# Experts' first layer: one 256-column operand for the high weights, halves added on VectorE, four PSUM banks in a ring

## The chip, the cores and the metric

One core of a Trainium2 chip runs the whole program. The metric is device time in microseconds; the program is launched once and its time is that of the core.

## The reference

Four transformer-like layers work on 2 sequences, 16 batches of 113 tokens with 256 features in all (1808 tokens). Only two of its parts are touched, the two mixtures of experts:

```python
# L0_ffn: 15 experts, 3 picks for each token, F = 256
logits = xt @ gate_w.T; scores = softmax(logits); topk_w, topk_idx = top_k(scores, 3)
h = einsum('td,efd->etf', xt, fc1_w) + fc1_b      # 512 outputs per expert
xh, g = h[..., :F], h[..., F:]
a = gelu(g, approximate=False) * xh * geglu_mult
yexp = einsum('etf,edf->etd', a, fc2_w) + fc2_b   # then weighted and summed over the picks
# L3_ffn: 8 experts, 1 pick, F = 1024
h = relu(xt @ w1[e] + b1[e]); y = h @ w2[e] + b2[e]
```

The kernel computes in pairs of fp16 numbers (a high part and the rest), three products for each product of the reference: high by high, high by low, low by high.

## The kernel before

`program` runs stage after stage; each is a block in which five engines run side by side, tied by semaphores, and a barrier stands between stages. A router stage sorts the tokens by expert into blocks of 128 rows, each of one expert. `stage_experts` then runs over the blocks. It is used twice: as m0x for L0 (57 blocks, NF = 4 chunks of 128 hidden units in the first layer, FH = 2 in the second, gelu, with the preparation of later weights, `PrepareShared`, laid beside it) and as m3x for L3 (23 blocks, NF = FH = 8, relu, no preparation).

For one block n:

- GpSimd (POOL) copies the block's row numbers (`idx`), gathers its 128 rows with an indirect DMA (`xg`, four buffers), and copies the expert's bias (`b1`, two buffers). It does so in a hardware loop, with registers in its waits.
- TensorE (PE) turns the gathered rows in four transposes into `pt` (`turn`), multiplies the first layer (`first`) into `ph` and the second (`second`) into `py`.
- ScalarE (ACT) copies `pt` to `xb` (`take_tokens`), makes `gate` from the upper half of `ph` with gelu (`take_gate`, m0x alone) and rounds the activation to fp16 (`high`; in m3x it reads `ph` with relu and bias).
- VectorE (DVE) makes the activation `a` from `ph` (`product`), the fp16 rest of it (`low`), and the output with its bias (`output`).
- SyncE (SP) fetches the output bias and stores the block's output to `m_out`.

The order on each engine is written out by hand. PE's in turn n is: turn(n+3), first(n+2), second(n). ACT's is, in m0x: high(n+1), take_tokens(n+3), take_gate(n+2), then a piece of the preparation; in m3x take_tokens(n+3), high(n+2). DVE's is: low(n+1), product(n+2), output(n), preparation (in m3x product(n+2), low(n+2), output(n)). So in m0x high(n+2) is the next thing that ACT does after take_gate(n+2), and `product(n+2)` on DVE stands between the two.

`ph` has two buffers of [128, NF, 128] floats. `first` waits for the xb of its block and for `taken` (a_ready or lo_ready) of the block two before. Its weights' place depends on the expert number, a value in a register, so each weight operand has an address that is worked out by the engine while it runs:

```python
def first(self, e, k, f):
    at, n = 2 * (k * self.NF + f) * 128, KC * self.NF * 256
    return [w[:].rearrange("p e k n -> p (e k n)").bitcast(mybir.dt.uint8)[:, bass.ds(e * n + at, 256)].bitcast(F16)
            for w in (self.w1_hi, self.w1_lo)]
```

Each f has two k steps (KC = 2), and `mm3` (lines 458 to 460) makes three matmuls of 128 columns for each: high weights by high tokens, high weights by low tokens, low weights by high tokens. Each matmul has a weight load of its own.

Of the kernel before, what the change touches and what calls it, by code (L numbers as in the profile page):

```python
# [6 lines left out]
F16 = mybir.dt.float16  # L7
I32 = mybir.dt.int32
U32 = mybir.dt.uint32
ALU = mybir.AluOpType  # L10
# [6 lines left out]
D = 256  # L17
# [139 lines left out]
class Ternary:  # L157
# [5 lines left out]
    def __init__(self, st, tag, mats, floor, depth):  # L163
# [5 lines left out]
        self.tot = st.ps(f"{tag}_tot", [128, M])  # L169
# [18 lines left out]
    def total(self, pe, i):  # L188
        pe.wait_ge(self.ones_set, 1)
        pe.wait_ge(self.summed, i + 1)  # L190
        pe.matmul(self.tot[:, i:i + 1], self.ones[:], self.asum[:, i:i + 1], start=True, stop=True).then_inc(self.totals, 1)

    def thresholds(self, dve, i):
        dram, out, scale = self.mats[i]
        dve.wait_ge(self.totals, i + 1)
        self.floor(dve, scale, self.tot[:, i:i + 1], 1.0 / (128 * dram.shape[1])).then_inc(self.scaled, 1)
# [92 lines left out]
class PrepareShared:  # L289
# [4 lines left out]
    def __init__(self, st, d, w, g):  # L294
# [6 lines left out]
                          lambda dve, out, tot, inv: dve.tensor_scalar(out, tot, inv, 1e-6, ALU.mult, ALU.add), 1)  # L301
# [19 lines left out]
    def on_tensor(self, pe, n):  # L321
        if n in (23, 40):
            self.bg.total(pe, (n - 23) // 17)
# [14 lines left out]
    def on_vector(self, dve, n):  # L338
# [16 lines left out]
        for i in range(2):  # L355
# [3 lines left out]
            if b == 5:  # L359
                self.bg.thresholds(dve, i)  # L360
# [1190 lines left out]
def stage_experts(nc, core, m, d, prepare=None):  # L1551
# [4 lines left out]

    N, NF, FH = m.blocks, m.NF, m.FH
    with Stage(nc, m.name + "x") as st:
# [3 lines left out]
        xb = [st.sb(f"xb{p}", [128, 2 * KC, 128], F16) for p in two]  # L1562
# [6 lines left out]
        ph = [st.ps(f"ph{p}", [128, NF, 128]) for p in two]  # L1569
        py = [st.ps(f"py{p}", [128, 512]) for p in two]  # L1570
        idx_ready, gathered, turned = ([st.sem(f"{n}{p}") for p in four] for n in ("idx_ready", "gathered", "turned"))
        xb_ready, h_ready, b1_ready, gate_ready, a_ready, hi_ready, lo_ready, y_ready, b2_landed, y_out, stored = (
            [st.sem(f"{n}{p}") for p in two] for n in (
                "xb_ready", "h_ready", "b1_ready", "gate_ready", "a_ready", "hi_ready", "lo_ready", "y_ready",
                "b2_landed", "y_out", "stored"))

        taken = a_ready if m.gelu else lo_ready
        if prepare is not None:
            prepare = prepare(st)
        with nc.Block() as block:  # L1580
            @block.gpsimd
            def _(pool):
# [3 lines left out]
                def gather(at):  # L1586
                    p, before = at.of(4)

                    wait_alone(pool, core, turned[p], before)
                    pool.tensor_copy(idx[p][:], m.ids[:, bass.ds(at.j, 1)]).then_inc(idx_ready[p], 1)  # L1590
                    wait_alone(pool, core, idx_ready[p], before + 1)
# [4 lines left out]
                def bias(at):  # L1596
                    p, before = at.of(2)
                    e = pool.value_load(m.expert[0:1, bass.ds(at.j, 1)], min_val=0, max_val=m.E - 1)

                    wait_alone(pool, core, taken[p], before)  # L1600
                    pool.tensor_copy(b1[p][:], m.b1[:, bass.ds(e, 1), :]).then_inc(b1_ready[p], 1)

                def step(at):
                    gather(at + 3)
                    bias(at)

                for n in range(3):
                    gather(At(0, n))
                steps(pool, N - 3, step)
                for n in range(N - 3, N):  # L1610
                    bias(At(0, n))

            @block.tensor
            def _(pe):
# [19 lines left out]
                def first(n, e):  # L1634
                    p = n % 2
                    pe.wait_ge(xb_ready[p], n // 2 + 1)

                    need(pe, taken[p], n // 2)
                    for f in range(NF):
                        for k in range(KC):  # L1640
                            last = mm3(pe, ph[p][:, f, :], *m.first(e, k, f), xb[p][:, k, :], xb[p][:, KC + k, :],
                                       k == 0, k == KC - 1)
                    last.then_inc(h_ready[p], 1)

                def second(n, e):
                    p, r = n % 2, n % 3

                    need(pe, y_out[p], n // 2)
                    pe.wait_ge(hi_ready[p], n // 2 + 1)
# [14 lines left out]
                for n in range(N):  # L1664
# [6 lines left out]
                    if prepare is not None:  # L1671
                        prepare.on_tensor(pe, n)

            @block.scalar
            def _(act):
                def take_tokens(n):
# [3 lines left out]
                    need(act, h_ready[p], n // 2)  # L1680
                    act.activation(xb[p][:].rearrange("p c n -> p (c n)"), pt[p][:, 0:2 * KC * 128],  # L1681
                                   ACT.Copy).then_inc(xb_ready[p], 1)

                def take_gate(n):
# [10 lines left out]
                def high(n):  # L1695
# [4 lines left out]
                    if m.gelu:  # L1700
                        act.wait_ge(a_ready[p], n // 2 + 1)
                        act.activation(a_hi[r][:], act32[p][:], ACT.Copy).then_inc(hi_ready[p], 1)
                        return
                    act.wait_ge(h_ready[p], n // 2 + 1)
                    act.wait_ge(b1_ready[p], n // 2 + 1)
                    for f in range(FH):
                        ins = act.activation(a_hi[r][:, f, :], ph[p][:, f, :], ACT.Relu, bias=b1[p][:, 0, f:f + 1])  # L1707
                    ins.then_inc(hi_ready[p], 1)

                take_tokens(0)  # L1710
                take_tokens(1)
                if m.gelu:
                    take_gate(0)
                    take_tokens(2)
                    high(0)
                    take_gate(1)
                else:
                    high(0)
# [1437 lines left out]
```

## Time and profile before

| | us |
|---|---|
| three runs | 1528.1, 1531.4, 1538.05 |
| median | 1531.4 |
| the profiled execution | 1543.3 |
| its span | 1541.6 |
| m0x within it, first to last store | 435.6 to 599.7 |
| m3x within it, first to last store | 1380.8 to 1511.3 |

Between the execution's time and its span lie 1.7 us. The profiled execution is 11.9 us, 0.8%, above the median. Of a page's engines, PE is TensorE's matmul and PEld its weight load; "idle before" is the time in which the engine waited, with what ended it. TensorE's granted clock is given as a share of 2.4 GHz, so 1.00 is 2.4 GHz and 0.50 is 1.2 GHz. A matmul's time in the profile runs to the end of its pipeline and overlaps the next one's; how fast matmuls follow each other is read from their starts.

### The profile page before, as it was taken

The page shows a single profiled execution, that of the slowest core. Times are in us where ns is not written, and L with a number is a line of the kernel's source. Part 1 is how long each engine was busy: PE and PEld are TensorE (multiplying, and loading weights), DVE is VectorE, ACT ScalarE, POOL GpSimd, SP SyncE. Part 2 cuts the span into 40 slices and gives each one's busy share as a digit, 9 for nine tenths or more (in the row PEclk, how much of TensorE's full clock was granted, in tenths as well). Part 3 has the DMA queues.
Part 4 walks back from the last instruction along what each step waited for, and adds up shares of the span by engine and source line. Part 5 has one row for each costly group of instructions (what it writes and reads, how often), then busy time and mean ns, then how long its engine had stood idle before and what let it go on. Part 6 is the DMA issues. An engine that isn't in the chain of part 4 may idle for free. (4 is left out here: it accounts for less than half of the span.)

```text
span 1541.6 us, 31533 instructions
## 1 busy us (share of the span) xinstructions
PE 1076.7 (70%) x9872; PEld 755.7 (49%) x9872; DVE 1068.9 (69%) x2356; ACT 697.0 (45%) x1392; POOL 489.6 (32%) x623
## 2 busy tenths in 40 slices
PE   4515887785199998676657867556569996479991
PEld 2212232224088885354444765334446664468881
DVE  3867999997645564565886764688768887745553
ACT  4505555553155553123425642234338887234440
POOL 0051777763145553730001100000015666232203
PEclk9557999996599999887777987678859998579996
DMA  6600000001154554312000000000013332112213
GB/s 209 205 3 11 1 1 0 1 1 43 50 151 134 162 135 152 95 42 82 1 1 1 1 1 0 0 1 0 0 43 108 115 112 70 49 46 67 64 51 119
DMA packets 47767, 89.68 MB, mean 58 GB/s; under 512 B 8353, under 2 KB 34630, under 8 KB 46790
## 3 DMA queue, kind: packets, MB, share of 16 engines
q1 hardware_dynamic: 40578, 67.98, 14.3%
q0 software_dynamic: 6912, 18.88, 4.4%
q8 instruction: 84, 1.38, 0.4%
q10 hardware_dynamic: 144, 1.05, 0.2%
q14 instruction: 49, 0.39, 0.1%
HBM read 71.84 MB, written 16.04 MB: 57 GB/s over the span
## 5 line engine op out<-in xcount | busy, mean ns | idle before, releaser
L909 POOL TENSOR_TENSOR scan_ch<-scan_hs,scan_ct 128x452 f32<-128x452 f32 x128 | 143.4, 1141 | 81.5 <-DVE scan_hs L1019 70.5
L932 PE MATMUL scan_py<-scan_ch,ident 128*128 128x452 f32 x256 | 130.8, 600 | 41.3 <-POOL scan_ch L909 31.6
L1019 DVE TENSOR_TENSOR_SCAN scan_hs<-scan_abar,scan_bx 128x452 f32<-128x452 f32 x128 | 132.8, 1077 | 0.9 <-ACT scan_abar L981 0.5
L458 PE MATMUL m0x_ph<-m0x_xb,m_w_hi 128*128 128x128 f16 x456 | 99.9, 221 | 0.6 <-ACT m0x_xb L1681 0.4
L459 PE MATMUL m0x_ph<-m0x_xb,m_w_hi 128*128 128x128 f16 x456 | 99.9, 221 | 0.0
L460 PE MATMUL m0x_ph<-m0x_xb,m_w_lo 128*128 128x128 f16 x456 | 99.4, 220 | 0.0
L1746 DVE TENSOR_SCALAR m3x_a<-m3x_ph,m3x_b 128x128 f32<-128x128 f32 x184 | 49.7, 343 | 68.6 <-ACT m3x_ah L1707 66.4
L932 PEld LDWEIGHTS scan_py<-scan_ch,ident 128*128 128x128 f32 x256 | 40.4, 192 | 112.7 <-POOL scan_ch L909 104.9
L981 ACT ACTIVATE scan_abar<-ssm_dt,ssm_a 128x448 f32<-128x448 f32 x128 | 80.8, 638 | 23.9 <-DVE scan_hs L1019 22.2
L1743 DVE SCALAR_TENSOR_TENSOR m0x_a<-m0x_ph,m0x_b,m0x_gate 128x128 f32<-128x128 f32 x114 | 34.7, 346 | 73.3 <-issue 39.9
L1707 ACT ACTIVATE m3x_ah<-m3x_ph,m3x_b 128x128 f16<-128x128 f32 x184 | 49.9, 382 | 64.9 <-PE m3x_ph L460 60.8
L2670 POOL MEMSET mha_v_hi<- 113x768 f16 x1 | 0.7, 737 | 243.3 <-POOLq L635 243.3
L2677 POOL TENSOR_TENSOR mha_prob_lo<-mha_prob,mha_prob_hi 113x452 f16<-113x452 f32 x64 | 65.5, 1046 | 38.0 <-ACT mha_prob_hi L2846 38.0
L458 PE MATMUL m3x_ph<-m3x_xb,m_w_hi 128*128 128x128 f16 x368 | 74.1, 224 | 2.8 <-DVE m3x_al L1757 2.4
L459 PE MATMUL m3x_ph<-m3x_xb,m_w_hi 128*128 128x128 f16 x368 | 74.2, 224 | 0.0
L460 PE MATMUL m3x_ph<-m3x_xb,m_w_lo 128*128 128x128 f16 x368 | 74.0, 223 | 0.0
L1011 DVE TENSOR_TENSOR scan_bx<-scan_pb,ssm_dx 128x452 f32<-128x452 f32 x128 | 72.8, 608 | 0.4 <-PE scan_pb L919 0.4
L1592 POOL DMA_INDIRECT m0x_xg<-m_rows,m0x_idx x57 | 55.6, 975 | 44.4 <-POOL m0x_idx L1590 42.5
L1828 POOL DMA_INDIRECT shared_got<-m_out,m_slot x48 | 51.4, 1071 | 36.1 <-issue 26.5
L976 ACT ACTIVATE scan_ct<-scan_pc 128x452 f32<-128x452 f32 x64 | 35.0, 547 | 60.1 <-POOL scan_ch L909 42.3
L1691 ACT ACTIVATE m0x_gate<-m0x_ph,m0x_b 128x128 f32<-128x128 f32 x114 | 35.6, 363 | 36.7 <-PE m0x_ph L460 25.0
L458 PE MATMUL m3x_py<-m_w_hi,m3x_ah 128*128 x184 | 50.1, 272 | 1.2 <-DVE m3x_yo L1764 0.8
(679 smaller groups left out, 3816.8 us busy)
## 6 DMA issues: line engine op xcount, KB each, us to landing
mha_wbuf<-m3w SPq DMA_DIRECT2D x32, 512.0 KB, 3.7
tok_wbuf<-m0w SPq DMA_DIRECT2D x15, 768.0 KB, 5.6
m0x_b<-m0b SPq DMA_DIRECT2D x57, 128.0 KB
m_out<-m0x_yo SPq DMA_DIRECT2D x57, 128.0 KB
m3x_b<-m3b SPq DMA_DIRECT2D x23, 128.0 KB, 3.0
m_out<-m3x_yo SPq DMA_DIRECT2D x23, 128.0 KB
m_rows<-m0r_parts SPq DMA_DIRECT2D x4, 448.0 KB
m_rows<-m3r_parts SPq DMA_DIRECT2D x4, 448.0 KB
```

The lines of the kernel that those rows point to most:

```text
L458: pe.matmul(out, w_hi, x_hi, start=start, stop=False)
L459: pe.matmul(out, w_hi, x_lo, start=False, stop=False)
L460: return pe.matmul(out, w_lo, x_hi, start=False, stop=stop)
L909: pool.tensor_tensor(ch[r][:], hs[r][:], ct[n % 2][:], ALU.mult).then_inc(weighed, 1)
L932: pe.matmul(py[c][:, 0:GT], core.ident[:], ch[u % R][:], start=n == 0, stop=n == NS - 1).then_inc(summed, 1)
L981: act.activation(abar[c][:, 0:GT].rearrange("p (b t) -> p b t", t=L)[:, :, 1:L], ssm.dt[:, c, cols].rearrange("p (b t) -> p b t", t=L)[:, ...
L1011: dve.tensor_tensor(bx[u % R][:], pb[n % 2][:, 0:GT], ssm.dx[:, c, cols], ALU.mult).then_inc(drive, 1)
L1019: dve.tensor_tensor_scan(hs[u % R][:], abar[c][:, 0:GT], bx[u % R][:], 0.0, ALU.mult, ALU.add).then_inc(scanned, 1)
L1592: pool.indirect_dma_start(xg[p][:], None, m.rows[:, :], bass.IndirectOffsetOnAxis(ap=idx[p][:, 0:1], axis=0)).then_inc(gathered[p], 16)
L1707: ins = act.activation(a_hi[r][:, f, :], ph[p][:, f, :], ACT.Relu, bias=b1[p][:, 0, f:f + 1])
L1828: pool.indirect_dma_start(self.got[j][k][:], None, m.out[:, :], bass.IndirectOffsetOnAxis(ap=m.slot[:, b, k:k + 1], axis=0)).then_inc(self ...
L2677: pool.tensor_tensor(prob_lo[g][:], prob[g % 2][:], prob_hi[g][:], ALU.subtract).then_inc(p_low, 1)
```

## The change

- **Operand.** `xb` is laid out as [part, k, token], so that the high and the low part of the tokens at one k are one operand of 2 x 128 columns. For each f, `first` makes four matmuls in place of six: high weights of k = 0 by both parts (256 columns), low weights of k = 0 and of k = 1 by the high part (128 columns each), high weights of k = 1 by both parts (256 columns). Columns in all stay the same (768 for each f), weight loads and matmuls go from 24 to 16 a block in m0x and from 48 to 32 in m3x.
- **Two halves.** The products with the low part of the tokens land in a half of their own, so each f takes [2, 128] floats of PSUM. A bank holds two f; there are four banks `ph0` to `ph3`, used in a ring. A block takes CP = NF/2 of them, 2 in m0x and 4 in m3x. A bank's `filled` is signalled after its two f; in m0x the gate's two f come first.
- **Adding the halves.** ACT copies the low half of each bank to SBUF (`take_low`, 256 columns a bank). DVE adds the high half from PSUM to it (`sums`), together with the bias where it can: in m0x one 256-column tensor_tensor for the gate's bank and two 128-column operations for the other; in m3x two 128-column operations for each of four banks. Before, DVE's `product` was two (m0x) or eight (m3x) 128-column operations. In m0x the gate's sum is what gelu now reads, from SBUF.
- **The product** of gate and activation in m0x (`multiply`) goes to POOL, one 256-column tensor_tensor of floats.
- **m3x's high** is one relu over 1024 columns of SBUF in place of eight of 128 columns of PSUM; **low** applies the relu again in its one operation.
- **POOL** has its blocks written out in place of the hardware loop; it gathers four blocks ahead instead of three, and its order in turn n is multiply(n), gather(n+4), bias(n+2).
- **Orders.** ACT in turn n: high(n+1), take_tokens(n+3), take_low(n+2), take_gate(n+2) (m0x alone), preparation. DVE in turn n: low(n+1), sums(n+2), output(n), preparation.
- The preparation's sums of weights use a spare column of `py` instead of a bank of their own, since all eight banks are taken; PE's step of it moves ahead of `second`, and DVE's thresholds come two turns earlier.

```diff
 def first(n, e):
     p = n % 2
     pe.wait_ge(xb_ready[p], n // 2 + 1)
-    need(pe, taken[p], n // 2)
-    for f in range(NF):
-        for k in range(KC):
-            last = mm3(pe, ph[p][:, f, :], *m.first(e, k, f), xb[p][:, k, :], xb[p][:, KC + k, :],
-                       k == 0, k == KC - 1)
-    last.then_inc(h_ready[p], 1)
+    order = list(range(FH, NF)) + list(range(FH)) if m.gelu else list(range(NF))
+    for i in range(CP):
+        b, uses = bank(n, i)
+        if uses:
+            before = n - BANKS // CP
+            pe.wait_ge(summed[before % 2], before // 2 * CP + i + 1)
+        for half in range(2):
+            f = order[2 * i + half]
+            both, high = ph[b][:, half, :, :], ph[b][:, half, 0, :]
+            (w0h, w0l), (w1h, w1l) = m.first(e, 0, f), m.first(e, 1, f)
+            pe.matmul(both, w0h, xb[p][:, :, 0, :], start=True, stop=False)
+            pe.matmul(high, w0l, xb[p][:, 0, 0, :], start=False, stop=False)
+            pe.matmul(high, w1l, xb[p][:, 0, 1, :], start=False, stop=False)
+            last = pe.matmul(both, w1h, xb[p][:, :, 1, :], start=False, stop=True)
+        last.then_inc(filled[b], 1)
...
+def take_low(n):                                   # ACT
+    p = n % 2
+    need(act, lo_ready[p], n // 2)
+    if m.gelu:
+        need(act, a_ready[p], n // 2)
+    for i in range(CP):
+        b, uses = bank(n, i)
+        dst = gate[p][:] if m.gelu and i == 0 else act32[p][:] if m.gelu else act32[p][:, 2 * i:2 * i + 2, :]
+        act.wait_ge(filled[b], uses + 1)
+        act.activation(dst, ph[b][:, :, 1, :], ACT.Copy).then_inc(copied[p], 1)
...
 def take_gate(n):                                  # ACT
     p = n % 2
-    act.wait_ge(h_ready[p], n // 2 + 1)
+    act.wait_ge(summed[p], n // 2 * CP + 1)
     act.wait_ge(b1_ready[p], n // 2 + 1)
-    need(act, a_ready[p], n // 2)
     for f in range(FH):
-        ins = act.activation(gate[p][:, f, :], ph[p][:, FH + f, :], ACT.Gelu,
+        ins = act.activation(gate[p][:, f, :], gate[p][:, f, :], ACT.Gelu,
                              bias=b1[p][:, 0, FH + f:FH + f + 1], scale=1.0 / WS)
     ins.then_inc(gate_ready[p], 1)
...
+def sums(n):                                       # DVE
+    p = n % 2
+    for i in range(CP):
+        b, uses = bank(n, i)
+        dve.wait_ge(copied[p], n // 2 * CP + i + 1)
+        if m.gelu and i == 0:
+            dve.tensor_tensor(gate[p][:], ph[b][:, :, 0, :], gate[p][:], ALU.add).then_inc(summed[p], 1)
+            continue
+        if i <= 1:
+            dve.wait_ge(b1_ready[p], n // 2 + 1)
+        for half in range(2):
+            f = half if m.gelu else 2 * i + half
+            ins = dve.scalar_tensor_tensor(act32[p][:, f, :], ph[b][:, half, 0, :], b1[p][:, 0, f:f + 1],
+                                           act32[p][:, f, :], ALU.add, ALU.add)
+        ins.then_inc(summed[p], 1)
...
+def multiply(n):                                   # POOL
+    p = n % 2
+    pool.wait_ge(summed[p], (n // 2 + 1) * CP)
+    pool.wait_ge(gate_ready[p], n // 2 + 1)
+    pool.tensor_tensor(act32[p][:], act32[p][:], gate[p][:], ALU.mult).then_inc(a_ready[p], 1)
```

## Rows read from the trace of the kernel before

**Rows 1.** Windows view, PE, PEld, DVE, ACT, POOL busy, PE clock, DMA share, GB/s.

```profile
436.00:590.00 154.00, 152.89 (x1775) 129.63 (x1773) 86.20 (x235) 83.00 (x216) 74.67 (x149) 1.00 0.49 140
1381.00:1507.00 126.00, 124.46 (x1491) 111.06 (x1489) 74.68 (x201) 53.87 (x178) 20.51 (x48) 1.00 0.21 60
```

**Rows 2.** Tile view of m_out: SyncE's stores, duration ns, first and last start us.

```profile
L1791 SPq DMA_DIRECT2D m_out<-m0x_yo x57: 316/351/402, 435.6 to 599.7; - x57
L1791 SPq DMA_DIRECT2D m_out<-m3x_yo x23: 348/355/366, 1380.8 to 1511.3; - x23
```

**Rows 3.** Timeline of m0x, PE alone: start us, duration us.

```profile
482.42 0.10 PEld L458 LDWEIGHTS m0x_ph<-m0x_xb,m_w_hi 128*128 x1
482.45 0.22 PE L458 MATMUL m0x_ph<-m0x_xb,m_w_hi 128*128 128x128 f16 x1
...
482.54 0.10 PEld L460 LDWEIGHTS m0x_ph<-m0x_xb,m_w_lo 128*128 x1
482.57 0.22 PE L460 MATMUL m0x_ph<-m0x_xb,m_w_lo 128*128 128x128 f16 x1
482.65 0.10 PEld L458 LDWEIGHTS m0x_ph<-m0x_xb,m_w_hi 128*128 x1
...
483.73 0.27 PE L460 MATMUL m0x_py<-m_w_hi,m0x_al 128*128 x1
...
483.84 0.27 PE L458 MATMUL m0x_py<-m_w_hi,m0x_ah 128*128 x1
```

**Rows 4.** Timeline of m3x: SyncE's stores of two blocks, PE within one block.

```profile
1380.77 0.35 SPq L1791 DMA_DIRECT2D m_out<-m3x_yo  x1
...
1421.41 0.22 PE L458 MATMUL m3x_ph<-m3x_xb,m_w_hi 128*128 128x128 f16 x1
...
1421.57 0.22 PE L458 MATMUL m3x_ph<-m3x_xb,m_w_hi 128*128 128x128 f16 x1
...
1422.68 0.22 PE L458 MATMUL m3x_ph<-m3x_xb,m_w_hi 128*128 128x128 f16 x1
...
1422.90 0.22 PE L458 MATMUL m3x_ph<-m3x_xb,m_w_hi 128*128 128x128 f16 x1
...
1424.93 0.27 PE L458 MATMUL m3x_py<-m_w_hi,m3x_ah 128*128 x1
...
1506.70 0.35 SPq L1791 DMA_DIRECT2D m_out<-m3x_yo  x1
```

**Rows 5.** Timeline of one m0x block, ACT and DVE; in brackets idle time and releaser.

```profile
483.53 0.62 ACT L1691 ACTIVATE m0x_gate<-m0x_ph,m0x_b 128x128 f32<-128x128 f32 x2 [0.61 <-PE m0x_ph L460]
484.19 0.61 DVE L1743 SCALAR_TENSOR_TENSOR m0x_a<-m0x_ph,m0x_b,m0x_gate 128x128 f32<-128x128 f32 x2 [1.26 <-issue]
...
484.89 0.42 ACT L1702 ACTIVATE m0x_ah<-m0x_a 128x256 f16<-128x256 f32 x1 [0.73 <-DVE m0x_a L1743]
...
485.22 0.58 ACT L1681 ACTIVATE m0x_xb<-m0x_pt 128x512 f16<-128x512 f16 x1
...
485.44 0.41 DVE L1757 TENSOR_TENSOR m0x_al<-m0x_a,m0x_ah 128x256 f16<-128x256 f32 x1
```

**Rows 6.** Groups by form, whole span: busy us, mean ns, idle before.

```profile
L2828 ACT ACTIVATE mha_v_hi<-mha_pvo 113x256 f16<-113x256 f32 x16 | 6.2, 385 | 0.0
L2289 DVE TENSOR_TENSOR h<-bgm_po,h 113x256 f32<-113x256 f32 x16 | 6.7, 419 | 6.8 <-PE bgm_po L2226 6.8
L909 POOL TENSOR_TENSOR scan_ch<-scan_hs,scan_ct 128x452 f32<-128x452 f32 x128 | 143.4, 1141 | 81.5 <-DVE scan_hs L1019 70.5 <-ACT scan_ct L976 8.8 <-PE scan_py L932 2.1
L735 POOL TENSOR_TENSOR h<-h,twice_prod 113x512 f32<-113x512 f32 x8 | 10.1, 1260 | 0.6
L185 DVE TENSOR_REDUCE m0x_bg_asum<-m0x_bg_buf 128x1 f32<-128x2048 f32 x2 | 4.6, 2276 | 0.0
L150 ACT ACTIVATE shared_s_hi<-m0x_s_h_f 128x1024 f16<-128x1024 f32 x2 | 2.1, 1056 | 0.0
L331 ACT ACTIVATE shared_s_hi<-m0x_s_f,m0x_gain 128x256 f16<-128x256 f32 x4 | 2.0, 506 | 0.0
```

**Rows 7.** Timeline of POOL at m0x's start, and of DVE and POOL later in it.

```profile
422.82 0.19 POOL L1601 COPY m0x_b<-m_b 128x4 f32 x1
...
424.85 0.20 POOL L1601 COPY m0x_b<-m_b 128x4 f32 x1
...
574.34 1.28 DVE L216 SCALAR_TENSOR_TENSOR bg_wp<-m0x_bg_buf,m0x_bg_thr,m0x_bg_neg 128x1024 f16<-128x1024 f32 x1
...
574.51 1.15 POOL L1590 COPY m0x_idx<-m_ids 128x1 uint32 x1
```

**Rows 8.** Timeline of one m3x block, DVE.

```profile
1420.80 2.16 DVE L1746 TENSOR_SCALAR m3x_a<-m3x_ph,m3x_b 128x128 f32<-128x128 f32 x8 [2.55 <-ACT m3x_ah L1707]
...
1423.00 1.22 DVE L1757 TENSOR_TENSOR m3x_al<-m3x_a,m3x_ah 128x1024 f16<-128x1024 f32 x1
```

**Rows 9.** Waits view of m3x: us in total, times, longest us.

```profile
PE m3x_ph L458 <- DVE m3x_al L1757: 2.4, 1, 2.4
```

**Rows 10.** Windows view, ten microseconds each, of two other stages; columns as in the first group.

```profile
740.00:750.00 10.00, 5.88 (x27) 5.43 (x28) 9.66 (x12) 1.79 (x4) 0.00 (x0) 0.50 0.00 0
...
1030.00:1040.00 10.00, 7.43 (x40) 4.79 (x38) 8.48 (x18) 4.31 (x8) 0.00 (x0) 0.83 0.01 2
```

More of the change, by code:

```diff
@@ L1561, in stage_experts @@
         xg = [st.sb(f"xg{p}", [128, D]) for p in four]
-        xb = [st.sb(f"xb{p}", [128, 2 * KC, 128], F16) for p in two]
+        xb = [st.sb(f"xb{p}", [128, 2, KC, 128], F16) for p in two]
         b1 = [st.sb(f"b1{p}", [128, 1, NF]) for p in two]
@@ L1594, in gather, with bias @@
                                             ).then_inc(gathered[p], 16)
[L1596 to L1600, printed above, removed]
-                    pool.tensor_copy(b1[p][:], m.b1[:, bass.ds(e, 1), :]).then_inc(b1_ready[p], 1)
[L1603 to L1611, printed above, removed]
+                def bias(n):
+                    p = n % 2
+                    e = pool.value_load(m.expert[0:1, n:n + 1], min_val=0, max_val=m.E - 1)
+                    need(pool, summed[p], n // 2 * CP)
+                    if m.gelu:
+                        need(pool, gate_ready[p], n // 2)
+                    pool.tensor_copy(b1[p][:], m.b1[:, bass.ds(e, 1), :]).then_inc(b1_ready[p], 1)
+                def multiply(n):
[3 more added lines that the diff above has]
+                    pool.tensor_tensor(act32[p][:], act32[p][:], gate[p][:], ALU.mult).then_inc(a_ready[p], 1)
+                for n in range(4):
+                    gather(n)
+                    if n < 2:
+                        bias(n)
+                for n in range(N):
+                    if m.gelu:
+                        multiply(n)
+                    if n + 4 < N:
+                        gather(n + 4)
+                    if n + 2 < N:
+                        bias(n + 2)
             @block.tensor
@@ L1701, in high @@
                         act.wait_ge(a_ready[p], n // 2 + 1)
[L1702 to L1708, printed above, removed]
+                    else:
+                        act.wait_ge(summed[p], (n // 2 + 1) * CP)
+                    act.activation(a_hi[r][:], act32[p][:], ACT.Copy if m.gelu else ACT.Relu).then_inc(hi_ready[p], 1)
                 take_tokens(0)
                 take_tokens(1)
+                take_low(0)
                 if m.gelu:
                     take_gate(0)
-                    take_tokens(2)
-                    high(0)
+                take_tokens(2)
+                take_low(1)
+                if m.gelu:
                     take_gate(1)
-                else:
-                    high(0)
-                    take_tokens(2)
-                    high(1)
+                high(0)
                 for n in range(N):
-                    if m.gelu and n + 1 < N:
+                    if n + 1 < N:
                         high(n + 1)
@@ L1726, in _ @@
                     if n + 2 < N:
-                        take_gate(n + 2) if m.gelu else high(n + 2)
+                        take_low(n + 2)
+                        if m.gelu:
+                            take_gate(n + 2)
                     if prepare is not None:
@@ L1765, in output @@
                                              ALU.add).then_inc(y_out[p], 1)
-                for n in range(-2, N):
-                    if m.gelu and 0 <= n + 1 < N:
+                sums(0)
+                sums(1)
+                low(0)
+                for n in range(N):
+                    if n + 1 < N:
                         low(n + 1)
                     if n + 2 < N:
-                        product(n + 2)
-                        if not m.gelu:
-                            low(n + 2)
-                    if n >= 0:
-                        output(n)
-                    if prepare is not None and n >= 0:
+                        sums(n + 2)
+                    output(n)
+                    if prepare is not None:
                         prepare.on_vector(dve, n)
```

83 lines of the change are left out of this document (43 added, 40 removed).

## The prediction

> **What bounds it now.** I read the busy shares by stage first, then each stage's period, then single blocks. In both expert stages TensorE is busy all the time at full clock: 152.9 of 154 us in m0x, 124.5 of 126 in m3x, while DVE and ACT are busy little over half of it [rows 1]. The stores give the period: in m0x (599.7 - 435.6)/56 = 2.93 us a block; in m3x 130.5/22 = 5.93 on average, which takes in the last two blocks, with no first layer beside them [rows 2]; without these it is (1506.70 - 1380.77)/20 = 6.30 [rows 4].
>
> "Busy" is not "at its peak", so I look at how matmuls follow each other. In m3x the first steps of `first` follow at 1421.57 - 1421.41 = 0.16 us for three matmuls of 128 columns, 0.055 each; later in the same block it is 1422.90 - 1422.68 = 0.22 [rows 4]. In m0x it is 482.65 - 482.42 = 0.23 all along, and the weight load of L460 starts at 482.54 although nothing of PE holds it [rows 3]. A matmul of 256 columns follows in 0.11 (483.84 - 483.73). So the second layer runs at the rate of its columns, and the first layer at that of its instructions: 0.06 us a step are lost because the next instruction isn't there yet. What comes late is either the instructions themselves (a load and its matmul are seen 0.03 apart, 482.42 and 482.45) or the address work between them.
>
> **PE's part.** Each f goes from 12 instructions (loads and matmuls) to 8, with the same columns and the same four addresses. Now it takes 0.45 us in m0x (two steps) and (1424.93 - 1421.41)/8 = 0.44 in m3x. Bounds: the columns alone are 6 x 0.055 = 0.33; if all of the lost 0.06 a step is address work, that isn't hidden by longer matmuls either, it stays 0.45. I take 0.03 for each of four instructions dropped, 0.12, and give 0.02 back for waits: 0.10 an f. That is 0.4 us a block in m0x (PE would need 2.5) and 0.8 in m3x. There four waits for banks are added; I count 0.65.
>
> The Trainium skill speaks against the gain: "TensorE: Matmul & The Clock Gate", section "Wait — 56ns, not 53.3ns?", has a matmul take its columns plus about 2.5 ns at full clock, whatever the decode path, so that eight fewer matmuls a block would give 0.02 us. The trace agrees on queued matmuls (0.055 and 0.11) and not on the 0.23 for three, which is why I don't take that as the answer.
>
> **m3x.** PE goes from 6.3 to about 5.65. Would another engine pass it? DVE: eight operations took 2.16 us [rows 8], as sums with their waits 2.5; before and after them stand high on ACT (1024 columns, 1.06, L150 [rows 6]) and low on DVE. low has its old size, 1.22 [rows 8]. These can form a loop, sums, high, low, sums: 2.5 + 1.06 + 1.2 + 0.2 = 5.0 us, under 5.65, so PE stays the bound. ACT has 1.06 + 0.6 + 4 x 0.385 = 3.2. The ring: first(n+2) needs the banks of block n+1, and PE spends 24 x 0.11 = 2.6 us on a second layer between the two firsts, while the sums of the earlier one need 2.5 from its first bank on; they are done in time. 20 periods x 0.65 = 13 us, and the one wait of 2.4 us for low before a first [rows 9] goes, since a bank is free after its sum: -15.4 us. Bounds: -2 (address work, the wait alone) and, at the columns' limit, 20 x 8 x 0.11 + 2.4 = -20.
>
> **m0x.** Here the other engines decide. ACT's present loop within a block is read from one [rows 5]: gate 0.62 (483.53), DVE's product 0.61 (484.19 to 484.80), high at 484.89, tokens at 485.22, ready for the next gate at 485.80; there it waits 0.6 us for PE. So today ACT and DVE together need 2.3 us a block and PE 2.93.
>
> After the change the same loop has more links, because high(n+2) is still what ACT does right after take_gate(n+2). From high's start:
> - high to tokens 0.33 (485.22 - 484.89), tokens to the copies 0.50 (0.58 less the overlap of two ACT instructions, 0.08 as between high and tokens);
> - first copy, 256 columns out of PSUM: 0.385 (L2828) [rows 6]; 0.08 to DVE (0.04 and 0.13 in rows 5: gate to product, high to low);
> - DVE's sum of the gate, 256 columns with one input in PSUM: 0.42 (L2289) [rows 6]; 0.09 back to ACT (484.80 to 484.89);
> - gate 0.62, read from SBUF; 0.06 to POOL;
> - POOL's product: 1141 ns for 452 columns and 1260 for 512 [rows 6]; the slope, 2.0 ns a column, gives 1141 - 196 x 2.0 = 0.75; in proportion it would be 0.64. I take 0.70; 0.09 back to ACT.
>
> Sum: 0.33 + 0.50 + 0.385 + 0.08 + 0.42 + 0.09 + 0.62 + 0.06 + 0.70 + 0.09 = 3.28 us. The second copy (0.3) and DVE's two 128-column sums (0.61, ending about when gelu does) lie beside this. DVE's own work is 0.42 + 0.61 + 0.42 + 0.41 = 1.9 us. POOL's: a gather and a bias took 2.03 us unhindered (424.85 - 422.82) [rows 7], plus 0.70 = 2.7; between the end of one product and the next gate's end ACT needs 2.5, POOL 2.0, so it just keeps up. PE needs 2.5. The loop over ACT, DVE and POOL is the bound, 3.28 against 2.93: 0.35 x 55 = +19 us.
>
> What lay beside PE's work is now on the path: ACT's preparation, 2.1 + 2.0 us (L150, L331) [rows 6] and about 0.4 for the shared bias, 4.5 us; of DVE's, two reductions of 2.28 us [rows 6] exceed the 1.5 us that DVE has free in a turn, +1.5; the other pieces (the longest is 1.28 [rows 7]) are covered by it. Filling and draining the stage each have the copy, the sum and POOL's product in place of DVE's: +1.2 twice. POOL's unrolled code and the moved `total` and thresholds I cost at nothing: POOL's waits are covered by its slack of 0.5 us, PE's step waits for a sum three turns old. The clock: PE will be at work 2.4 of 3.3 us. A stage where it was busy 7.4 of 10 us was granted 0.83, one with 5.9 was granted 0.50 [rows 10]; a block at 1.2 GHz takes 2 x 2.2 = 4.4 us, but PE has first(n+2) done some 1.7 us before ACT asks for it, which takes up one such block. I count +3. m0x: 19 + 4.5 + 1.5 + 2.4 + 3 = +30.4. Bounds: loop 3.15 and half the preparation hidden +15; half of all blocks at 1.2 GHz +50.
>
> POOL and DVE: a 128x1 copy that takes 0.19 us took 1.15 next to a 1.28 us DVE operation on SBUF [rows 7]. The Trainium skill has a rule for it ("SBUF — State Buffer", section "Who interferes with whom"): the two share a port pair that one instruction holds as a whole, a DVE operation with two SBUF inputs shutting out GpSimd's reads. The trace agrees. In the steady loop DVE has only PSUM work while POOL multiplies, so this hits the preparation's turns alone, within the bounds.
>
> **Sum.** 30.4 - 15.4 = +15 on the profiled execution, 1543.3 to 1558.3 (span 1541.6 to 1556.6). That execution stood 0.8% over the median of its runs; the difference should carry over to the median, 1531.4 + 15 = 1546.
>
> **The rivals.**
> - *PE stays m0x's bound*, because the loop isn't one (the wait for POOL's product falls beside other ACT work, or links are shorter than their nearest rows). Then m0x gains with PE, to 2.65 a block, -15, and with m3x it is 1531.4 - 30 = 1501. For it: ACT busy is only 83 of 154 us now. Against: the order of calls leaves nothing between take_gate and high, and today's 0.73 us wait of ACT at that very place [rows 5].
> - *The first layer gets no faster on PE* (addresses are what is late). m3x then gives back only its 2.4 us: 1531.4 + 30 - 2 = 1559. For it: four address calculations an f stay. Against: they would have to fill the whole 0.06 us.
> - *m0x falls to the low clock or to late rows*: the loop leaves PE gaps of 0.9 us a turn, the clock is granted at 0.5 for many blocks, and each such block costs up to 4.4 - 3.3 = 1.1 us beyond the first. It decides from about every third block on: 57 x 0.4 = +23 more, 1569; at every block 1600. The Trainium skill's "TensorE: Matmul & The Clock Gate", section "A second HAM failure mode: psum-queue depth-cycling", tells of just such a loss with banks used in turn and short idle spots; in this trace the expert stages ran at 1.00 throughout their steady part [rows 1].
>
> **How the numbers follow.** What I forecast has a chance of 0.60 and, with its bounds (+15 to +50 and -20 to -2), lies between 1526 and 1579; its middle lies just inside 1% (15.3 us, about what a measurement of this kernel tells from no change), so I split it 0.02 faster, 0.36 same, 0.22 slower. PE stays the bound: 0.13, faster. No gain on PE: 0.12, 0.10 of it slower. Low clock: 0.15, slower. Faster 0.15, same 0.38, slower 0.47. The range leaves out most of the fast rival and the upper half of the slow one: 1518 to 1580.
>
> **What would show it.** In m0x's steady part: stores 3.3 us apart; PE busy near 0.75 of it; ACT waiting 0.8 to 0.9 us before each high, released by POOL's a, and 0.3 before each gate, released by DVE's sum; POOL's product near 0.70. In m3x: stores about 5.65 apart, matmul starts of one f within 0.35 us, PE busy all the time. I am wrong if ACT waits for PE before its copies in m0x (the first or third rival: the clock in the window says which) or if an f in m3x still takes 0.44.

## The result and the profile after

After: 1558.67 us, median of four runs (1554.15 to 1561.63), against 1532.21 for before (four runs, 1528.10 to 1538.05). The ratio is 1.0162, 95% interval 1.0124 to 1.0200: 1.6% slower; the medians lie 26.5 us apart. The profiled execution took 1557.89 us, with a span of 1556.1.

SyncE's stores again give the periods (tile view of m_out; duration ns, first and last start us):

```profile
L1840 SPq DMA_DIRECT2D m_out<-m0x_yo x57: 343/351/366, 436.2 to 632.4; - x57
L1840 SPq DMA_DIRECT2D m_out<-m3x_yo x23: 349/355/366, 1395.5 to 1526.4; - x23
```

m0x: 196.2/56 = 3.50 us a block, where it was 2.93 [rows 2]. m3x: 130.9/22 = 5.95, where it was 5.93: no block got shorter. From a stage's first instruction to its last store, m0x grew by 31.7 us (185.1 to 216.9) and m3x shrank by 5.4 (158.0 to 152.6), all of the latter outside the run of blocks. The sum, +26.3, is what the medians show. The two profiled executions themselves lie only 14.6 us apart (1543.3 and 1557.9), since in the second the rest of the program took 12 us less; the first experiment is about that.

The windows (us; PE, PEld, DVE, ACT, POOL busy; clock; DMA share; GB/s), against [rows 1]:

```profile
436.00:620.00 184.00, 163.00 (x1350) 119.55 (x1348) 104.73 (x284) 114.74 (x318) 115.69 (x206) 0.99 0.42 118
1396.00:1521.00 125.00, 124.82 (x1189) 106.19 (x1187) 76.60 (x200) 62.62 (x118) 19.78 (x48) 1.00 0.22 61
```

In m0x PE now idles 21 of 184 us at a nearly unchanged clock (0.99, before 1.00), and nobody else is full either: that is a loop of engines that wait for each other. In m3x PE is as full as before with a fifth fewer matmuls (1189, not 1491). The waits of m0x name the loop's links (us in total, times, longest):

```profile
ACT m0x_ah L1753 <- POOL m0x_a L1628: 56.1, 50, 2.0
...
POOL m0x_a L1628 <- ACT m0x_gate L1740: 51.2, 51, 1.3
...
ACT m0x_gate L1740 <- DVE m0x_gate L1786: 11.6, 50, 0.6
```

Read the loop off one block (timelines of ACT, then DVE, then POOL; start, duration; idle time before and its releaser in brackets), against [rows 5]. L1753 is `high`, the cast to fp16; L1721 `take_tokens`; L1733 `take_low`, the copy; L1786 the gate's sum; L1740 the gelu; L1628 the product; L338 a piece of preparation:

```profile
479.47 0.42 ACT L1753 ACTIVATE m0x_ah<-m0x_a 128x256 f16<-128x256 f32 x1 [0.56 <-POOL m0x_a L1628]
479.80 0.58 ACT L1721 ACTIVATE m0x_xb<-m0x_pt 128x512 f16<-128x512 f16 x1
480.27 0.38 ACT L1733 ACTIVATE m0x_gate<-m0x_ph 128x256 f32<-128x256 f32 x1
...
481.14 0.69 ACT L1740 ACTIVATE m0x_gate<-m0x_gate,m0x_b 128x128 f32<-128x128 f32 x2 [0.22 <-DVE m0x_gate L1786]
481.74 0.49 ACT L338 ACTIVATE shared_s_hi<-m0x_s_f,m0x_gain 128x256 f16<-128x256 f32 x1
482.80 0.42 ACT L1753 ACTIVATE m0x_ah<-m0x_a 128x256 f16<-128x256 f32 x1 [0.56 <-POOL m0x_a L1628]
```

```profile
480.68 0.42 DVE L1786 TENSOR_TENSOR m0x_gate<-m0x_ph,m0x_gate 128x256 f32<-128x256 f32 x1 [0.34 <-ACT m0x_gate L1733]
```

```profile
481.98 0.72 POOL L1628 TENSOR_TENSOR m0x_a<-m0x_a,m0x_gate 128x256 f32<-128x256 f32 x1 [0.99 <-ACT m0x_gate L1740]
```

From cast to cast, 479.47 to 482.80, it is 3.33 us: tokens at 0.33, copy 0.47 later, 0.38 for it, 0.03 to DVE, 0.42 sum, 0.04 back, 0.69 gelu, 0.15 to POOL, 0.72 product, 0.10 back. ACT's piece of preparation (L338) lies in the wait for POOL.

The trace gives the same for the stage. Of its 56 turns from cast to cast, the 40 with an undisturbed product take 3.34 us on average. The 16 in which POOL's product took longer than its usual 0.73 us take 3.89, in all 9.0 us more than 3.33 a turn.

In m3x the matmuls of one f step start so (PE's timeline), against [rows 4]:

```profile
1440.50 0.27 PE L1680 MATMUL m3x_ph<-m3x_xb,m_w_hi 128*128 128x256 f16 x1
1440.61 0.27 PE L1677 MATMUL m3x_ph<-m3x_xb,m_w_hi 128*128 128x256 f16 x1
1440.72 0.22 PE L1678 MATMUL m3x_ph<-m3x_xb,m_w_lo 128*128 128x128 f16 x1
1440.84 0.22 PE L1679 MATMUL m3x_ph<-m3x_xb,m_w_lo 128*128 128x128 f16 x1
1440.95 0.27 PE L1680 MATMUL m3x_ph<-m3x_xb,m_w_hi 128*128 128x256 f16 x1
```

Each starts 0.11 us after the one before, whether that had 256 columns or 128. Four take 0.45 us (1440.95 - 1440.50), what six took before (0.44 to 0.45).

### The profile page after: what moved, and what is told of

Its sections match the earlier page's. It is cut to its first block and busy times, and to the rows that moved or that the text cites. A ratio compares the mean times of both kernels' runs of the same rounds, so it can differ in the third digit from the quotient of the medians.

```text
span 1556.1 us, 29740 instructions
## 1 busy us (share of the span) xinstructions
PE 1085.2 (70%) x9048; PEld 735.5 (47%) x9048; DVE 1094.6 (70%) x2413; ACT 742.2 (48%) x1437; POOL 532.4 (34%) x679
## 3 DMA queue, kind: packets, MB, share of 16 engines
q8 instruction: 78, 1.28, 0.3%
## 5 line engine op out<-in xcount | busy, mean ns | idle before, releaser
L1677 PE MATMUL m0x_ph<-m0x_xb,m_w_hi 128*128 128x256 f16 x228 | 63.1, 277 | 16.0 <-ACT m0x_xb L1721 13.2
L1628 POOL TENSOR_TENSOR m0x_a<-m0x_a,m0x_gate 128x256 f32<-128x256 f32 x57 | 50.4, 884 | 69.1 <-ACT m0x_gate L1740 66.7
L1792 DVE SCALAR_TENSOR_TENSOR m3x_a<-m3x_ph,m3x_b,m3x_a 128x128 f32<-128x128 f32 x184 | 54.7, 345 | 25.5 <-ACT m3x_a L1733 25.3
L1803 DVE TENSOR_TENSOR m0x_al<-m0x_a,m0x_ah 128x256 f16<-128x256 f32 x57 | 25.0, 438 | 62.8 <-ACT m0x_ah L1753 56.5
L1680 PE MATMUL m0x_ph<-m0x_xb,m_w_hi 128*128 128x256 f16 x228 | 62.4, 274 | 0.4
L1733 ACT ACTIVATE m3x_a<-m3x_ph 128x256 f32<-128x256 f32 x92 | 35.2, 384 | 37.3 <-PE m3x_ph L1680 34.9
L1753 ACT ACTIVATE m0x_ah<-m0x_a 128x256 f16<-128x256 f32 x57 | 23.7, 416 | 60.0 <-POOL m0x_a L1628 60.0
L1677 PE MATMUL m3x_ph<-m3x_xb,m_w_hi 128*128 128x256 f16 x184 | 50.7, 276 | 0.1
L1680 PE MATMUL m3x_ph<-m3x_xb,m_w_hi 128*128 128x256 f16 x184 | 50.5, 275 | 0.0
L467 PE MATMUL m3x_py<-m_w_hi,m3x_al 128*128 x184 | 50.1, 272 | 0.0
L1678 PE MATMUL m0x_ph<-m0x_xb,m_w_lo 128*128 128x128 f16 x228 | 50.1, 220 | 0.0
```

What stands on the lines that cost most here:

```text
L1628: pool.tensor_tensor(act32[p][:], act32[p][:], gate[p][:], ALU.mult).then_inc(a_ready[p], 1)
L1677: pe.matmul(both, w0h, xb[p][:, :, 0, :], start=True, stop=False)
L1680: last = pe.matmul(both, w1h, xb[p][:, :, 1, :], start=False, stop=True)
L1792: ins = dve.scalar_tensor_tensor(act32[p][:, f, :], ph[b][:, half, 0, :], b1[p][:, 0, f:f + 1], act32[p][:, f, :], ALU.add, ALU.add)
```

## The experiments

The theory after this comparison: in m3x, PE's pace is that of the weight addresses, each an addition in a register on PE's sequencer, and the merged operand saves none; in m0x the loop over ACT, DVE and POOL is the bound. The rivals: columns or weight loads set the 0.11 us; the surplus of m0x comes from gathers that are late. On the chips of these runs before took 1543 to 1545 us (1529 in the last), so ratios are compared.

**A second profile of before.**

> The kernel before, unchanged, profiled a second time. The two traces at hand differ by +31.7 us in the m0x stage, -5.4 us in m3x and -12.3 us in everything between and around them, 8.7 us of that in the shared experts' stage (119.7 before, 111.0 after), which the change touches only through what is prepared for it. Theory: the first profile of before was a long one outside the two stages (its own time was 11 us above its median), so this one shows m0x 187.4 and m3x 161.2 within 1 us each and the rest of the program some 10 us shorter, about 740 us. Rival: the shared stage really gains from the change; then the rest is 751 us again, and the 26.5 us of the medians is 31.7 - 5.4 with a further loss elsewhere that must be found.

Measured: 1545.8 us, m0x 185.3 and m3x 158.9 us by the same reading, so both stages repeat within 1 us. The rest of the program took 1200 us, in the first profile 1198: the expectation of a shorter one fell. In fourteen profiles that rest ranges from 1180 to 1205 us with no relation to what was changed in the stages. The first profile of after has 1187, well inside that range. So nothing shows the shorter shared stage of after to be a gain of the change, and of single profiles I compare the two stages' lengths alone.

**The new stage for m3x only.**

```
-            stage_experts(nc, core, moe3, d)
+            stage_experts_new(nc, core, moe3, d)      # the function of after; m0x keeps the old one
```

> The new stage for m3x only, m0x as before. Theory (each weight address worked out in a register costs PE's sequencer about 0.11 us, so that four matmuls of an f step take the 0.45 us that six took): m3x loses 5.4 us, all in the first and last blocks, and the period of a block stays 6.30 us; the program gains 5 us, a ratio of 0.9965. Rival (the prediction's sum): 0.65 us a block, 15.4 us, ratio 0.990. Second rival: the 5.4 us was noise of one profile; ratio 1.000.

Measured: ratio 0.9936, interval 0.9911 to 0.9962; the stage 152.5 us, 5.5 to 6.4 less than in the two profiles of before; 130.6 us between first and last store as before. The interval excludes the prediction's 15.4 us (0.990), but the expected 0.9965 lies just outside it as well: 0.9936 is 9.9 us, of which the stage accounts for 5.5 to 6.4. For the rest I have no account. It is the best version of this study.

**Constant weight addresses in the first layer**, in after and in before.

```
# after so changed
-  (w0h, w0l), (w1h, w1l) = m.first(e, 0, f), m.first(e, 1, f)
+  (w0h, w0l), (w1h, w1l) = m.first(0, 0, f), m.first(0, 1, f)
# before so changed
-  last = mm3(pe, ph[p][:, f, :], *m.first(e, k, f), ...)
+  last = mm3(pe, ph[p][:, f, :], *m.first(0, k, f), ...)
```

> The kernel after, with expert 0 named as a constant in the addresses of the first layer's weights (left out: that a block uses its own expert there; the second layer still does), so that no register is computed ahead of those matmuls. Theory of the addresses: an f step of four matmuls falls from 0.45 us to the time of its columns, 768 at about 2.4 per ns = 0.32 us; m3x, bound by PE, falls by 8 x 0.12 = 1.0 us a block, to about 5.3, or to what ACT needs if that is more; m0x, bound by the loop through ACT, DVE and POOL, keeps its 3.3 to 3.5 us a block. Rival (the columns or the array's own weight loads set the 0.11 us between matmuls): both periods and the 0.45 us stay as they are.

> The kernel before, with expert 0 named as a constant in the first layer's weight addresses (left out: that a block uses its own expert in that layer). The same edit of after brought m3x's period from 6.26 to 5.47 us. Theory (the addresses hide everything else; with them gone an f step of six 128-column matmuls takes the time of its 768 columns, as four with the same columns do): period 5.5 here too, so that merging two operands gives nothing even where no address is in the way. Rival (the prediction's view: each of the two matmuls saved is worth 0.03 to 0.06 us): 5.47 + 8 x 2 x 0.03 = 5.95 or more.

The first fence is of after so changed, the second of before so changed; PE's timelines in m3x:

```profile
1450.08 0.27 PE L1677 MATMUL m3x_ph<-m3x_xb,m_w_hi 128*128 128x256 f16 x1
1450.19 0.22 PE L1678 MATMUL m3x_ph<-m3x_xb,m_w_lo 128*128 128x128 f16 x1
1450.25 0.22 PE L1679 MATMUL m3x_ph<-m3x_xb,m_w_lo 128*128 128x128 f16 x1
1450.30 0.27 PE L1680 MATMUL m3x_ph<-m3x_xb,m_w_hi 128*128 128x256 f16 x1
1450.41 0.27 PE L1677 MATMUL m3x_ph<-m3x_xb,m_w_hi 128*128 128x256 f16 x1
```

```profile
1450.58 0.22 PE L458 MATMUL m3x_ph<-m3x_xb,m_w_hi 128*128 128x128 f16 x1
...
1450.92 0.22 PE L458 MATMUL m3x_ph<-m3x_xb,m_w_hi 128*128 128x128 f16 x1
```

An f step is 0.33 us in the one (four matmuls) and 0.34 in the other (six): the columns' time, 0.055 for 128 and 0.11 for 256. The median spacing of m3x's stores is 5.47 and 5.51 us. So the addresses were what held both kernels, and with them gone the merge is worth 0.04 us a block. m0x kept 3.48 us in after, as a loop outside PE must; in before it fell from 2.93 to 2.72. PE idles there, 14.8 us of the stage in waits for DVE's `low`: the next loop stands 0.2 us a block below the addresses. The two programs took 1556.4 and 1506.7 us, one execution each.

**The merge alone undone.** Each 256-column matmul becomes two, their weights' address shared.

```
-  pe.matmul(both, w0h, xb[p][:, :, 0, :], start=True, stop=False)
+  pe.matmul(ph[b][:, half, 0, :], w0h, xb[p][:, 0, 0, :], start=True, stop=False)
+  pe.matmul(ph[b][:, half, 1, :], w0h, xb[p][:, 1, 0, :], start=False, stop=False)
...   # and so for w1h
```

> The kernel after with the merged operand alone undone: each 256-column matmul of the first layer is two of 128 columns with the same weights, so six matmuls an f step again, four weight addresses as in both kernels; the ring of banks, the sums on DVE and all else stay. Theory (the addresses set PE's pace in the first layer, and six matmuls of 768 columns fit behind four of them): m3x's period stays 6.26 us, m0x's 3.50, the stage lengths within 1 us of after's, ratio to before 1.016 as after. Rival (fewer matmuls did help, by 0.03 us each as the prediction took): m3x 6.26 + 16 x 0.03 = 6.7 us a block, the program 10 us slower than after, ratio 1.022.

Measured: ratio 1.0180 (1.0129 to 1.0231), store spacing 6.30 us (median) in m3x and 3.50 (mean) in m0x, against after's 6.26 and 3.50. Sixteen matmuls more a block cost 0.04 us in m3x, where the rival, at the prediction's 0.03 each, had 0.5. The theory held.

**More addresses.** Before, with an address of its own for the second matmul of each three in m3x.

```
+  again = nc.s_assert_within(e & 15, ...)
-  mm3(pe, ph[p][:, f, :], *m.first(e, k, f), xb[p][:, k, :], xb[p][:, KC + k, :], k == 0, k == KC - 1)
+  (w_hi, w_lo), (w_hi2, _) = m.first(e, k, f), m.first(again, k, f)
+  # three matmuls as before, the second with w_hi2
```

> The kernel before, with more addresses in m3x and nothing else: the second of the two matmuls that share a high weight no longer shares its address, but gets one worked out anew from the masked expert number. 16 address additions and 2 register operations more a block (69 for 51), the same 76 matmuls with the same data. Theory (PE's sequencer does its register operations one after the other and they are what m3x's and m0x's periods consist of: 6.27 us by 51 and 2.93 by 24 are both 0.12 us each): m3x's period grows by 18 x 0.12 = 2.2 us to 8.4 to 8.5 us, an f step from 0.45 to 0.68 us, m0x stays 2.93. Rival (the address of a matmul is worked out behind the matmuls queued ahead, so that only the order of four in a row matters): under 7.2 us. The interleaved kernels, whose period stayed 6.27, fit the theory: mixing the two layers changes no number of register operations.

Measured: 1569.4 us beside 1528.9 for before. Median spacing in m3x 8.33 us, in m0x 2.93. PE's timeline:

```profile
1450.57 0.22 PE L1645 MATMUL m3x_ph<-m3x_xb,m_w_hi 128*128 128x128 f16 x1
1450.68 0.22 PE L1646 MATMUL m3x_ph<-m3x_xb,m_w_lo 128*128 128x128 f16 x1
1450.79 0.22 PE L1644 MATMUL m3x_ph<-m3x_xb,m_w_hi 128*128 128x128 f16 x1
1450.90 0.22 PE L1645 MATMUL m3x_ph<-m3x_xb,m_w_hi 128*128 128x128 f16 x1
```

Every 128-column matmul now starts 0.11 us after the last; in before two of three shared an address and came in pairs. The price is (8.33 - 6.31)/18 = 0.112 us a register operation. The times are one execution each, so the period carries the result.

The traces also hold direct evidence that the views above leave out: a record for each register operation and each semaphore wait of PE's sequencer. They follow each other in 0.11 us, beside the matmuls of the second layer as of the first. In m3x a block of before, and of after, has 53 of them (50 register operations, one of them a fused one, and three waits). In 15 blocks no two are more than 0.28 us apart, so the sequencer is at work all through the block. 53 x 0.1125 = 5.96 us, and five or six longer pauses a block add 0.38: 6.34 for a period of 6.3. In this run it is 70 records and 0.47 of pauses, 8.35 for 8.3; in m0x of before 25 and 0.18, 2.99 for 2.96. With constant addresses 21 are left in m3x, with up to 3.3 us between two. What the pauses are stays open.

This also explains the 0.16 us of the block's first step in [rows 4]. The addresses of that step were worked out while the matmuls queued ahead were running, 0.6 us before their own matmuls started; the matmuls then catch up, and at 1422.68 the address is 0.09 us ahead. The sequencer's own pace is 0.11 us an operation in both places.

**The two layers interleaved**, in m3x and then in both stages.

```
-  first(n + 2, e[n + 2])
-  second(n, e[n])
+  # y_out, hi and lo of block n awaited first; then, for each f (in m0x each second f):
+  #   the matmuls of first(n + 2) for this f, then mm3 of second(n) for its f
```

> The new stage for m3x alone, with PE's two layers interleaved: behind each f step of the first layer of block n+2 the matching f step of the second layer of block n. Until now they ran one after the other: 8 x 0.45 us with the addresses late, then 24 matmuls of 256 columns in 2.6 us, in which two addresses each are early. Theory: one kind covers the other, and a block costs the larger of its 48 addresses and 3 register operations at 0.11 us (5.7) and its columns, 5.3 us: period 5.8, 20 x 0.45 = 9 us off m3x_alone, ratio to before 0.988. Rival (the queue ahead of PE already evens this out, or is too short to): 6.2 us, ratio 0.993.

> As m3x_interleave, and the same interleaving in m0x's old stage: behind f 1 and f 3 of block n+2 the two f steps of block n's second layer. Addresses in m0x: 20 and 4 register operations, 24 x 0.1125 = 2.7 us of a period of 2.93. Theory: 2.93 falls to 2.75 to 2.8, 8 us of the program, ratio to before 0.983. Rival (the second layer's low part, which is ready 1.25 us (median) ahead of the block's transposes, is now needed 2 us earlier than before, and is late wherever preparation runs): m0x no faster or some us slower, ratio 0.988 to 0.992.

Measured: ratios 0.9996 (0.9974 to 1.0018) and 1.0011 (0.9983 to 1.0040). m3x's spacing stayed 6.27 and 6.26 us: the theory's 5.8 fell. That fits a sequencer that is busy all through the block, with the register operations of both layers in line, so that their order doesn't matter; its records are again never more than 0.28 us apart. The filling also lost the 5 us that the new stage had won (first store 26.7 us after the stage's start, not 21.9), since block 0's second layer now ends with block 2's first (it takes 7.6 us from its first matmul to its last, not 2.8). The expected ratios, 0.988 and 0.983, did not come either. m0x went to 3.04 us a block, slower, as the rival had it; which of the earlier waits does it wasn't taken apart.

**m0x: the order of gathers.**

```
                 for n in range(N):
+                    if n + 4 < N:
+                        gather(n + 4)
                     if m.gelu:
                         multiply(n)
-                    if n + 4 < N:
-                        gather(n + 4)
```

> The kernel after, with one thing moved on POOL: the gather of block n+4 is issued ahead of the product of block n, not behind it. In the trace of before, a gather is issued 9.4 us (median) ahead of the transposes that use it and lands 3.1 to 5.0 us after its issue; in that of after it is issued 3.8 us ahead, since POOL waits for the gelu and multiplies first. Theory A (the late gathers are the surplus of m0x over the bare ACT loop: mean period 3.50, undisturbed 3.31): the mean falls to 3.31, 10 us, ratio to before 1.010. Theory B (the ACT loop alone is late, the gathers' waits lie in its shadow): no gain, 1.016, or a small loss where the gather's 1.3 us on POOL delay the product.

Measured: ratio 1.0178 (1.0112 to 1.0243), mean period 3.47. A gather was issued 6.8 us (median) ahead of its use, not 3.8, and PE's waits for gathers were gone from the list; that bought 0.03 us a block. Theory B held: late gathers weren't the surplus. POOL's product still took over 0.8 us in 16 of 57 blocks, 9.2 us in all over its median of 0.73 (9.1 in after). One such block, DVE and POOL of after, where the product runs beside a DVE instruction of the preparation:

```profile
470.66 1.21 DVE L154 SCALAR_TENSOR_TENSOR shared_s_lo<-m0x_s_h_f,shared_s_hi 128x1024 f16<-128x1024 f32 x1
```

```profile
470.77 1.69 POOL L1628 TENSOR_TENSOR m0x_a<-m0x_a,m0x_gate 128x256 f32<-128x256 f32 x1 [0.99 <-ACT m0x_gate L1740]
```

**m0x: the order on ACT and DVE.**

```
 # ACT, turn n (order of the calls)
-high(n+1), take_tokens(n+3), take_low(n+2), take_gate(n+2)
+take_tokens(n+3), take_low(n+2), high(n+1), take_gate(n+2)
 # DVE, turn n
-low(n+1), sums(n+2), output(n)
+sums(n+2), low(n+1), output(n)
```

> The kernel after, with m0x's turn on ACT in another order: token copy of n+3, the two low-half copies of n+2, the cast of n+1, then the gelu of n+2; on DVE the sums of n+2 ahead of the low part of n+1. The copies then run while POOL multiplies block n+1 and the DVE sum of n+2 lies under the cast, so neither of ACT's two waits (0.56 for POOL, 0.22 for DVE) remains. Theory (in m0x the ACT turn with its waits is what is late): the period falls from 3.50 us to PE's 2.93 us; 55 x 0.5 = 28 us, ratio to before about 0.998 (0.993 to 1.003). Rival (ACT's busy time alone sets it: 2.1 us of instructions, 0.5 of preparation and the gaps between): a period of 3.1 to 3.2, ratio 1.006 to 1.01. Second rival (the long link is POOL's product, 0.73 to 1.75 us, wherever it stands): 3.4 us, 1.013.

Measured: ratio 1.0096 (1.0064 to 1.0127); median spacing 3.03 us, mean 3.26. The expected 2.93 us and 0.998 did not come; the ratio is the one that the first rival (ACT's own work is the bound) had. Yet the loop is gone, and no product was stretched (0.72 to 0.73 in all). What is late next is the gather, still issued behind the product, 4.3 us ahead of its use (waits from 440 to 595 us):

```profile
PEld m0x_pt L1659 <- DMA m0x_xg<-m_rows,m0x_idx: 13.6, 16, 4.7
...
PE m0x_pt L1659 <- DMA m0x_xg<-m_rows,m0x_idx: 9.2, 9, 4.4
```

**m0x: the product on DVE**, alone and with the order above.

```
-  pool.tensor_tensor(act32[p][:], act32[p][:], gate[p][:], ALU.mult).then_inc(a_ready[p], 1)
+  dve.tensor_tensor(act32[p][:], act32[p][:], gate[p][:], ALU.mult).then_inc(a_ready[p], 1)   # behind output(n)
```

> The kernel after, with m0x's product taken from POOL to DVE, behind DVE's output of the turn. It takes the 0.73 to 1.75 us product with its way through POOL off the loop and puts one DVE instruction of about 0.42 us in its place; POOL is left with gathers and biases, so these are early again. ACT's order is unchanged. Theory: the loop falls from 3.31 to about 2.95 to 3.0 us, level with PE's 2.93, and the 0.19 of late gathers goes; 55 x 0.5 = 27 us, ratio to before 0.998. Rival (DVE becomes the bound: it is busy 58% of the stage and gets 0.42 us of 3 more, with preparation on top): a period of 3.2, ratio 1.008.

> Both edits of m0x together: the product on DVE and ACT's order with the copies of n+2 ahead of the cast of n+1. With the order alone the period was 3.26 (median 3.03), and PE then waited 27 us in 160 for gathers. Theory (ACT's waits and late gathers are the whole loss of m0x): period 2.93 to 2.95, PE's own; together with m3x's gain, ratio to before 0.994 to 0.996. Rival (preparation and DVE set it): 3.05, ratio 1.000.

Measured: ratios 1.0050 (1.0014 to 1.0085) and 0.9978 (0.9944 to 1.0011). Their stores:

```profile
L1844 SPq DMA_DIRECT2D m_out<-m0x_yo x57: 343/351/366, 436.2 to 608.2; - x57
```

```profile
L1848 SPq DMA_DIRECT2D m_out<-m0x_yo x57: 343/351/366, 437.4 to 602.7; - x57
```

3.07 and 2.95 us a block. The first has the shorter links and early gathers; its 1.0050 lies between its theory (0.998) and its rival (1.008). The second has no loop as well, and is back at PE's 2.93. Its ACT does the same work in the same order as under the new order alone, so ACT's work was not what held that kernel at 3.26. Its ratio is a little above the expected 0.994 to 0.996, which the interval takes in, as it does the rival's 1.000; the period decides between them. Gathers are issued 6.5 and 7.0 us ahead. With both edits the change's loss in m0x is gone to 1 us, but nothing is won there: PE still does 24 register operations a block.

## Why the prediction came out as it did

The forecast was +15 us (1546, range 1518 to 1580); measured +26.5. The sign, the stage and the mechanism of the loss were right; the gain that should have paid for half of it did not come. For the profiled execution the forecast was 1558.3 and the measurement 1557.9. That is luck: the rest of the program, which the forecast left as it was, took 12 us less in that execution than in before's.

*PE's part: this step failed.* "I take 0.03 for each of four instructions dropped" gave, less 0.02 for waits, 0.10 us an f. An f costs 0.45 us before and after; sixteen matmuls more a block cost 0.04 us, and 16 addresses with 2 other register operations 2.0. The text named the right bound ("if all of the lost 0.06 a step is address work ... it stays 0.45") and had the evidence: in [rows 3, 4] a step of three matmuls with two addresses takes 0.22 to 0.23, which is 2 x 0.112. Dividing the step by its addresses, not by its instructions, would have found it. The Trainium skill's rule that spoke against the gain ("TensorE: Matmul & The Clock Gate", section "Wait — 56ns, not 53.3ns?": columns plus some 2.5 ns) put the worth of eight matmuls fewer at 0.02 us; the pairs measured here, 5.47 against 5.51 and 6.26 against 6.30, are 0.04 for sixteen. I had set it aside because of the 0.23, which it wasn't about.

*m3x.* Forecast -15.4, measured -5.4. The 13 us from periods were 0; the 2.4 for the wait of [rows 9] came, and 3 more that I hadn't counted. In m3x_alone the first `second` starts 2.6 us earlier after the stage's start than in before (that wait), 1.5 more are gained until the last one ends (0.8 of it a wait for yo in before), and the last store follows it by 0.5, not 1.9 us. The first fits the hand-over by banks: the wait of [rows 9] is gone from the list. The last two I read from the traces and tested no further.

*m0x.* Forecast +30.4, measured +31.7. The loop's links summed to 3.28; they measure 3.33, link by link within 0.09. That makes 0.40 x 56 = 22 us. The other 11.4 forecast (preparation on ACT and DVE, filling, clock) were 9 us, of another kind: ACT's preparation lay in its wait for POOL (a turn with 1.04 us of it took 3.32), the clock stayed at 0.99, and POOL's product was stretched by DVE's preparation, 9.1 us, which I had left "within the bounds". So the stage's total came close in part by luck. "POOL just keeps up" was right as far as ACT goes; that its gathers lost most of their lead (9.4 us to 3.8) I didn't foresee. It cost nothing until the loop was opened, and about 0.3 us a block then (3.26 against 2.95 with the product on DVE).

*The rivals.* "The first layer gets no faster on PE" gave 1559 at a chance of 0.12; that is what happened (1558.67), by its named mechanism. To the tenth it is luck: the four executions spread over 7 us, and m3x gave back 5 us where it had 2. PE did not stay m0x's bound, and the low clock did not come (its 1600 at every block would be 1606 by its own terms; nothing rests on it). *What would show it*: an f in m3x still at 0.44 was named as the sign of error, and is what the profile shows. ACT's wait before the gate was 0.2 for a forecast 0.3, before the cast 1.1 on average, stretched products included, for a forecast 0.8 to 0.9, the product 0.725 for 0.70.

## What to carry to other kernels

Before merging matmuls, find what the sequencer does between them: where the operand's address comes from a register, count additions, not matmuls or instructions, and try one build with constant addresses to see what the columns alone would take. When an edit moves a product to another engine, write the loop it closes in order and sum it against the bound; then ask which queued transfers on that engine now stand behind a wait. Read the ends of a stage apart from its period: here they gained 5.4 us in m3x though no block got shorter.

## What the runs showed of the hardware

- A register operation on PE's sequencer takes 0.112 us, whichever matmuls run beside it, and where the sequencer is the slower part each one lengthens the period by that: m3x with 51 and 69 of them a block takes 6.31 and 8.33 us. A semaphore wait that is already met takes a like time there (0.11 to 0.13). A 256-column matmul and two of 128 take the same 0.11 us.
- POOL's 128x256 product took 0.73 us alone, 1.69 beside a DVE instruction of 1.21 us with two SBUF inputs and up to 1.75 beside one of 1.28. The Trainium skill states that such a DVE instruction contends with a GpSimd instruction that reads SBUF ("SBUF — State Buffer", section "Who interferes with whom"); the trace agrees, at up to 1.0 us each time. A DVE tensor_scalar of 128x1024 with one SBUF tensor for input (0.74 us, L211) did it as well: 1.22 us for the product, four times.
- POOL's gap from the index copy to the gather was 0.75 us in the rolled loop of before and 0.27 in the unrolled code of after. Both changed together with the waits' form, so which of the two it is stays open.
